# Cross-attention and FFN on one core: loads for attention behind those of query weights, the residual inside the output sums

## The chip, the cores and the metric

The kernel runs on one core of one Trainium2 chip. Its time is the device time in microseconds, lower is better. The core has the engines PE (TensorE, matmuls), DVE (VectorE), ACT (ScalarE), POOL (GpSimd) and SP (SyncE, which here issues every DMA). They run beside each other, each through its own list of instructions in order, and wait for each other on semaphores.

## The reference

B = 8 sequences of 128 tokens of width D = 512, a context of the same shape, 32 heads of width 128:

```
h   = layernorm(x)                      # mean and variance of each token
x1  = x + h + attention(rmsnorm(h) * ln_weight, context) @ w_out.T
        # scores = q k^T + position_bias[head], masked; softmax; times v
n   = layernorm(x1)
out = x1 + ((n * in_scale) @ sign(W).T) * out_scale + bias
        # in_scale, out_scale: softmax(n @ gate.T) times two tables of 8 rows
```

All is float32. The residual x + h of a token is x * (1 + rstd) - mean * rstd: one multiplication with res_scale = 1 + rstd and one addition of res_shift = -mean * rstd.

## The kernel before

**Projections.** A matrix of weights in float32 is split into a high and a low part (w_hi, w_lo; ACT makes the high one, DVE or POOL the low one), and so are the activations (c_hi, c_lo for the context, x_hi, x_lo for the input). A product of two tiles is then three matmuls (L1237, L1238, L1239): high by high, low by high, high by low. Keys and queries come in 16 pairs of heads each, values in 16 pieces. These 48 groups stand in a fixed order, first keys and values mixed, at its end four value pieces (numbers 24 to 27), the last four key pairs (28 to 31), then the 16 query pairs (32 to 47). Except for the first two, a group is a 2 by 2 block product computed with 7 products instead of 8 (a Strassen-like scheme). It needs sums of weight tiles (step WS, on POOL, L695 to L700) and sums of activation tiles (T1 to T4, steps CT and XT, on DVE), and it adds the seven products up in a ring of tiles in SBUF with E1 and C11 (ACT, L760 and L764) and E6, E65, C22, C12, C21 (DVE, L947 to L965). One product is two times three matmuls of 128 x 512.

The input x is loaded and normalised, transposed on PE into big_stage, and then summed and split: steps XT (T3, T1, T2, T4: L1026 to L1035) and XX i (x_hi by ACT at L840, x_lo by DVE at L1079). The split of 4 reads T4, and T4 overwrites what the split of 7 reads.

**Loads.** SP walks its own list. WL m, r is one of two 256 KB loads of the weights of pair m (m = 16 is the first query pair; L565). It waits until the tiles that it overwrites have been read: by the sums of pair m - 1 on POOL, by w_lo of pair m - 1, parts 0 and 1 (row 0), and by part 3 of pair m - 2 (row 1). SAVE writes a ring tile of keys or values to HBM (L599, L602), 256 KB each. KV p loads the keys and the values of head pair p back, 1 MB each (L632, L635); BL i loads the position bias of a head, 64 KB (L643); WOL p loads the output weights of a pair, 512 KB (L650); AL loads x again into acc, 2 MB in all (L655); SMALL loads the FFN's bias, tables and gate (L659 to L662), after POOL has cleared two tiles (L727, L728). All of them go through one hardware queue over 16 DMA engines.

**Attention.** For half a batch and one head (a unit, 64 in all): scores S on PE (L1309); DVE adds bias and mask and takes the maximum (L1101, L1104; the sum of bias and mask is BM, on POOL, L717); EXP on ACT (L846); N normalises on DVE (L1109 to L1111); T transposes on PE (L1317) and ACT copies (L854); PV multiplies with the values on PE (L1328) and splits the result on ACT and DVE (L864, L1118). For each pair of heads p, OUT p, b multiplies the result for sequence b with the output weights, and DVE adds it to acc (add_out, L1127). WO p splits these output weights: the high part on ACT (L872), the low part on POOL (L723). PE writes the outputs into two banks in turn; an output waits until the addition of the output before the last has been made. Projections of query pair p + 2 and attention of pair p are interleaved on PE.

**The residual.** RES b (residual, L1085) turns acc[b] from x into x * res_scale + res_shift, eight instructions of 128 x 512 on DVE. The first additions wait for all eight.

**The order.** schedule() writes one list of steps by hand. Every engine walks the same list and takes the steps that concern it, so the list fixes the order on each engine, and a step of one engine that is placed early can block what stands behind it. Products of group n and of group n - 1 alternate: in cycle n, slots 0, 2, 4, 6 hold the products 1, 6, 2, 5 of group n and slots 1, 3, 5 hold the products 7, 3, 4 of group n - 1. put(cycle, slot, ...) places other steps behind the product of a slot. In the diff k = 24 is the group of the first of the last four value pieces, so k + 5, k + 6, k + 7 are key groups 29, 30, 31, and q = 32 is the first query group. Behind cycle q + 1 the list goes on by head pairs; its first part (p == 0) is written out. WL 16 stands in slot 0 of cycle k + 7, WL 17 in slot 0 of cycle q, WL 18 in slot 0 of cycle q + 1.

Of the kernel before, what the change touches and what calls it, by code (L numbers as in the profile page):

```python
# [82 lines left out]
def schedule():  # L83
# [3 lines left out]
    def put(cycle, slot, *found):  # L87
        beside.setdefault((cycle, slot), []).extend(found)
# [79 lines left out]
    put(k + 4, 5, ("XT", "T2"), ("XX", 7))  # L168
    put(k + 5, 1, ("XX", 6))
    put(k + 5, 4, ("XX", 3))  # L170
    put(k + 5, 6, ("XX", 5))
    put(k + 6, 2, ("XT", "T4"), ("XX", 4))
    put(k + 6, 5, ("KV", 0), ("BL", 0), ("BL", 1))
    q = at[QUERIES[0]]
    put(q, 5, ("BM", 0), ("BM", 1))
    put(q, 6, ("KV", 1), ("WOL", 0))

    put(q + 1, 0, ("S", 0), ("EXP", 0), ("SMALL",))
    put(q + 1, 3, ("N", 0), ("BL", 2))
    put(q + 1, 4, ("S", 1))  # L180
    put(q + 1, 6, ("T", 0), ("EXP", 1), ("BM", 2))

    def product(n, i):
        return [("P", n, i), (READ[i], n)] + ([("SAVE", n, READ[i])] if n < NKV and READ[i] in RESULT else [])
# [52 lines left out]
    for p in range(SPLIT // 2):  # L237
# [8 lines left out]
        if p == 0:  # L246

            first = q + 1
            steps += [*product(first, 7), *prod[1], ("WX", m, 2), ("N", 1), ("PV", 0), ("RES", 0), ("RES", 1)]
            steps += [("S", 2), *product(first, 3), ("T", 1), ("EXP", 2), ("BM", 3), ("BL", 3), *prod[6], ("N", 2), ("PV", 1),  # L250
                      ("WO", 0), ("RES", 2), ("RES", 3)]
            steps += [("S", 3), *product(first, 4), *prod[2], ("WX", m, 3), ("T", 2), ("EXP", 3), ("BM", 4), *prod[5], ("N", 3),
                      ("PV", 2), ("WOL", 1), *load, ("RES", 4), ("RES", 5)]
            steps += [("S", 4), *prod[7], *prod[3], ("T", 3), ("EXP", 4), ("BM", 5), ("BL", 4), ("RES", 6), ("RES", 7), *prod[4],
                      *outs(0, 0), ("N", 4), ("KV", 2), *sums, ("PV", 3), *outs(0, 1, 2)]
            continue
# [32 lines left out]
def xattn_ffn(nc, x, ctx_t, mask, pos_bias, ln_w, wq, wk, wv, wo, ffn_w, ffn_bias, gate_t, scales, out):  # L289
# [27 lines left out]
    with ExitStack() as ctx:  # L317
# [6 lines left out]
        def sem(name):  # L324
            return ctx.enter_context(nc.semaphore(name))
# [99 lines left out]
        v_last_res, v_n, v_scales = sem("v_last_res"), sem("v_n"), sem("v_scales")  # L425
        v_vsum, v_vs4, v_xsum, v_res, v_start = sem("v_vsum"), sem("v_vs4"), sem("v_xsum"), sem("v_res"), sem("v_start")

# [508 lines left out]
        def _(dve):  # L936
# [143 lines left out]

            def residual(i):

                dve.wait_ge(d_acc, 16 * (i // HALF + 1))
                dve.wait_ge(v_res, 4)
                dve.tensor_scalar(acc[:, i, :], acc[:, i, :], res_scale[:, i:i + 1], res_shift[:, i:i + 1],  # L1085
                                  ALU.mult, ALU.add).then_inc(v_start, 1)

            def masks():
# [31 lines left out]
            def add_out(p, b):  # L1120
                n = nth_out[p, b]
                dve.wait_ge(pe_out, n)
                if p:
                    dve.wait_ge(v_acc, nth_out[p - 1, b])
                else:
                    dve.wait_ge(v_start, B)
                dve.tensor_tensor(acc[:, b, :], out_bank[n % 2][:], acc[:, b, :], ALU.add).then_inc(v_acc, 1)  # L1127
# [71 lines left out]
            def scale_product(i):  # L1199
# [6 lines left out]
                if i == B - 1:  # L1206
# [6 lines left out]
                  "CT": ctx_sum, "CX": ctx_low, "LN": input_statistics, "RMS": mean_squares, "RMSR": rms_reciprocals, "H": normed,  # L1213
                  "XT": x_sum, "XX": x_low, "RES": residual, "MASK": masks, "S": scores, "N": normalise,
                  "PV": out_low, "OUT": add_out, "ST": ffn_statistics, "LN2": ffn_norms, "LS": normal_scales, "NT": normal_tile,
# [226 lines left out]
```

## Time and profile before

| | us |
|---|---|
| median of 3 runs (870.11 to 871.13) | 870.71 |
| the profiled execution's own time | 868.79 |
| its span, first to last instruction | 867.0 |
| PE busy | 842.7 |
| DVE busy | 634.1 |

The mean granted clock of PE is 0.985 of full speed. An engine's rows give start, duration and what it did; in brackets stands how long the engine was idle before, and what released it. PE rows of consecutive matmuls overlap, since matmuls are pipelined: the distance from start to start is the time that one takes. Times are microseconds from the start of the span.

### The profile page before, as it was taken

Reading aid. Unit: us, or ns where it says so; the run is one execution under the profiler, and the core shown is the slowest. Engines: PE = TensorE matmul, PEld = TensorE weight load, DVE = VectorE, ACT = ScalarE, POOL = GpSimd, SP = SyncE. Lnnn points to the kernel's source line nnn. Section 1 sums busy time; section 2 is a strip of 40 time slices with the busy share of each in tenths; the row PEclk is TensorE's granted clock in tenths of the full one; section 3 lists DMA queues with packets and bytes.
Section 4 is the critical chain, followed back from the end, with each engine's and each line's share of the span. In section 5 each row is a group of like instructions: output and inputs, shape, how many; then the busy total and the mean of one; then the engine's idle time right before and its main releaser. Section 6 shows DMA issues by size and latency. Waiting matters only on the chain.

```text
span 867.0 us, 12861 instructions
## 1 busy us (share of the span) xinstructions
PE 842.7 (97%) x4348; PEld 705.9 (81%) x4348; DVE 634.1 (73%) x1019; ACT 390.2 (45%) x1005; POOL 302.1 (35%) x279
## 2 busy tenths in 40 slices
PE   9999999999999979989999999999999999999887
PEld 8778888888888858778888888888888888888775
DVE  5777845868765955877778677777777786789765
ACT  5532513422522523535544554455455445556642
POOL 2103211112210233525435544544554345433236
PEclk9999999999999999999999999999999999999969
DMA  8364464663453666123134214412431342150002
GB/s 268 132 212 170 152 208 142 204 220 132 146 180 110 216 229 226 60 106 108 70 131 149 97 60 152 149 62 95 149 113 70 125 150 98 58 208 7 1 1 97
DMA packets 60576, 114.07 MB, mean 132 GB/s; under 512 B 5192, under 2 KB 38600, under 8 KB 55264
## 3 DMA queue, kind: packets, MB, share of 16 engines
q1 hardware_dynamic: 60512, 113.25, 37.9%
q8 instruction: 36, 0.59, 0.3%
q14 instruction: 28, 0.23, 0.1%
HBM read 77.58 MB, written 35.65 MB: 131 GB/s over the span
## 4 chain that ended last, share of the span: by engine, by line
PE 84%; DVE 8%; issue 3%; DMA 2%; ACT 2%; SPq 1%; POOL 0%; DVEq 0%; POOLq 0%; ACTq 0%
PE out L1237 9%; PE out L1239 9%; PE out L1238 9%; PE proj L1237 8%; PE proj L1239 8%; PE proj L1238 8%; PE o L1328 6%; PE s L1309 6%; PE s L1237 3%; PE s L1238 3%; PE s L1239 3%; PE t L1317 3%; DMA w_stage<-in_wq 2%; PE proj L1395 1%; PE proj L1396 1%
## 5 line engine op out<-in xcount | busy, mean ns | idle before, releaser
L846 ACT ACTIVATE probs<-probs,neg_max 128x128 f32<-128x128 f32 x256 | 99.7, 391 | 141.2 <-DVE neg_max L1104 141.1
L695 POOL TENSOR_TENSOR w_stage<-w_stage 128x256 f32<-128x256 f32 x30 | 25.3, 844 | 320.8 <-DMA w_stage<-in_wk 131.3
L1127 DVE TENSOR_TENSOR acc<-out,acc 128x512 f32<-128x512 f32 x128 | 87.4, 688 | 43.0 <-PE out L1239 42.7
L707 POOL TENSOR_TENSOR w_lo<-w_stage,w_hi 128x512 fp32r<-128x512 f32 (+1 forms) x52 | 59.3, 1150 | 142.4 <-ACT w_hi L784 142.4
L1237 PE MATMUL proj<-x_hi,w_hi 128*128 128x512 f32 x210 | 89.9, 428 | 9.6 <-DVE w_lo L972 4.2
L1237 PE MATMUL out<-wo_hi,o_hi 128*128 128x512 f32 x224 | 95.3, 426 | 0.7 <-DVE acc L1127 0.6
L1239 PE MATMUL out<-wo_lo,o_hi 128*128 128x512 f32 x224 | 88.2, 394 | 0.0
L1238 PE MATMUL out<-wo_hi,o_lo 128*128 128x512 f32 x224 | 87.6, 391 | 0.0
L1239 PE MATMUL proj<-x_lo,w_hi 128*128 128x512 f32 x210 | 83.6, 398 | 0.0
L1238 PE MATMUL proj<-x_hi,w_lo 128*128 128x512 f32 x210 | 83.0, 395 | 0.0
L717 POOL TENSOR_TENSOR bias_mask<-bias_raw,mask_neg 128x512 f32<-128x512 f32 x64 | 76.8, 1210 | 9.7 <-DVE probs L1101 9.0
L784 ACT ACTIVATE w_hi<-w_stage 128x512 fp32r<-128x512 f32 (+1 forms) x113 | 61.6, 566 | 23.3 <-DMA w_stage<-in_wq 8.5
L1111 DVE TENSOR_TENSOR probs<-probs,inv_sum 128x512 f32<-128x512 f32 x64 | 67.3, 1051 | 2.2
L864 ACT ACTIVATE o_hi<-o 128x512 fp32r<-128x512 f32 x60 | 35.7, 595 | 48.7 <-PE o L1328 48.7
L1118 DVE TENSOR_TENSOR o_lo<-o,o_hi 128x512 fp32r<-128x512 f32 x60 | 41.0, 683 | 20.7 <-ACT o_hi L864 20.7
L1237 PEld LDWEIGHTS proj<-x_hi,w_hi 128*128 128x128 f32 x210 | 40.1, 191 | 16.9 <-issue 4.6
L972 DVE TENSOR_TENSOR w_lo<-w_stage,w_hi 128x512 fp32r<-128x512 f32 (+1 forms) x61 | 40.9, 670 | 17.2 <-ACT w_hi L784 16.5
L1239 PEld LDWEIGHTS out<-wo_lo,o_hi 128*128 128x128 f32 x224 | 42.0, 188 | 9.6
L1237 PEld LDWEIGHTS out<-wo_hi,o_hi 128*128 128x128 f32 x224 | 42.5, 190 | 7.8 <-issue 1.9
L846 ACT ACTIVATION_READ_ACCUMULATOR probs<-probs,neg_max 128x1 f32 x256 | 47.9, 187 | 0.0
L1239 PEld LDWEIGHTS proj<-x_lo,w_hi 128*128 128x128 f32 x210 | 40.0, 190 | 9.3
L1238 PEld LDWEIGHTS out<-wo_hi,o_lo 128*128 128x128 f32 x224 | 42.5, 190 | 6.0
(317 smaller groups left out, 2143.8 us busy)
## 6 DMA issues: line engine op xcount, KB each, us to landing
k_spill<-ring SPq DMA_DIRECT2D x64, 256.0 KB, 2.7
v_spill<-ring SPq DMA_DIRECT2D x64, 256.0 KB, 2.2
w_stage<-in_wk SPq DMA_DIRECT2D x32, 256.0 KB, 3.4
big_stage<-in_wv SPq DMA_DIRECT2D x8, 1024.0 KB, 7.6
k_first<-k_spill SPq DMA_DIRECT2D x8, 1024.0 KB, 7.3
v_first<-v_spill SPq DMA_DIRECT2D x8, 1024.0 KB, 4.9
w_stage<-in_wq SPq DMA_DIRECT2D x32, 256.0 KB, 4.4
k_second<-k_spill SPq DMA_DIRECT2D x8, 1024.0 KB, 6.7
```

The source lines that it names most:

```text
L707: pool.tensor_tensor(lo, staged(m, part), hi.bitcast(F32), ALU.subtract).then_inc(g_wlo, 1)
L717: pool.tensor_tensor(bias_mask[:, j % 2], bias_raw[:, i % 2][:, None, :].to_broadcast([P, HALF, P]), mask_neg[:, halves[half], :], ALU.add ...
L784: act.activation(hi, staged(m, part), ACT.Copy).then_inc(a_whi, 1)
L846: last = act.activation(probs[:, j % 2, b, :], probs[:, j % 2, b, :], ACT.Exp, bias=neg_max[:, col:col + 1], accum_out=row_sum[:, col:col ...
L1111: dve.tensor_tensor(probs[:, j % 2], probs[:, j % 2], inv_sum[:, cols, None].to_broadcast([P, HALF, P]), ALU.mult).then_inc(v_probs, 1)
L1118: dve.tensor_tensor(lo[:, h % 2], o_bank[:], hi[:, h % 2].bitcast(F32), ALU.subtract).then_inc(v_olo, 1)
L1127: dve.tensor_tensor(acc[:, b, :], out_bank[n % 2][:], acc[:, b, :], ALU.add).then_inc(v_acc, 1)
L1237: pe.matmul(to[:], left_hi, right_hi, start=first and n == 0, stop=False, skip_group_check=True)
L1238: pe.matmul(to[:], left_lo, right_hi, start=False, stop=False, skip_group_check=True)
L1239: last = pe.matmul(to[:], left_hi, right_lo, start=False, stop=n == len(pairs) - 1, skip_group_check=True)
L1309: last = pe.matmul(to[:, b * P:(b + 1) * P], queries[:, b * P:(b + 1) * P], keys, start=True, stop=True)
L1328: last = pe.matmul(to[:, b * P:(b + 1) * P], v_tiles[p % 2][:, half * HALF + b, i * P:(i + 1) * P], probs_t[:, j % 2, b * P:(b + 1) * P], ...
```

## The change

- T4 goes from slot 2 of cycle k + 6 to slot 3 of cycle k + 5, and the split that reads it (XX 4) from slot 2 to slot 1 of cycle k + 6.
- KV 0 and the first two bias loads go from slot 5 of cycle k + 6 to slot 1 of cycle k + 7: behind WL 16, and the bias loads first.
- KV 1 goes from slot 6 of cycle q, in front of WOL 0 and WL 18, to slot 1 of cycle q + 1, behind both.
- WO 0, the split of the first output weights, goes from behind PV 1 to slot 3 of cycle q + 1.
- SMALL goes from slot 0 of cycle q + 1 to behind PV 0.
- The eight RES steps go. add_out for p == 0 is acc * res_scale + output and for p == 1 (output + res_shift) + acc, one scalar_tensor_tensor each; it waits for the load of acc and the four scale and shift instructions in place of the eight residuals.

```diff
--- before.py
+++ after.py
@@ -167,16 +167,19 @@
     put(k + 4, 2, ("XT", "T1"), ("XX", 2))
     put(k + 4, 5, ("XT", "T2"), ("XX", 7))
     put(k + 5, 1, ("XX", 6))
+    put(k + 5, 3, ("XT", "T4"))
     put(k + 5, 4, ("XX", 3))
     put(k + 5, 6, ("XX", 5))
-    put(k + 6, 2, ("XT", "T4"), ("XX", 4))
-    put(k + 6, 5, ("KV", 0), ("BL", 0), ("BL", 1))
+    put(k + 6, 1, ("XX", 4))
+
+    put(k + 7, 1, ("BL", 0), ("BL", 1), ("KV", 0))
     q = at[QUERIES[0]]
     put(q, 5, ("BM", 0), ("BM", 1))
-    put(q, 6, ("KV", 1), ("WOL", 0))
-
-    put(q + 1, 0, ("S", 0), ("EXP", 0), ("SMALL",))
-    put(q + 1, 3, ("N", 0), ("BL", 2))
+    put(q, 6, ("WOL", 0))
+
+    put(q + 1, 0, ("S", 0), ("EXP", 0))
+    put(q + 1, 1, ("KV", 1))
+    put(q + 1, 3, ("N", 0), ("BL", 2), ("WO", 0))
     put(q + 1, 4, ("S", 1))
     put(q + 1, 6, ("T", 0), ("EXP", 1), ("BM", 2))
 
@@ -246,12 +249,11 @@
         if p == 0:
 
             first = q + 1
-            steps += [*product(first, 7), *prod[1], ("WX", m, 2), ("N", 1), ("PV", 0), ("RES", 0), ("RES", 1)]
-            steps += [("S", 2), *product(first, 3), ("T", 1), ("EXP", 2), ("BM", 3), ("BL", 3), *prod[6], ("N", 2), ("PV", 1),
-                      ("WO", 0), ("RES", 2), ("RES", 3)]
+            steps += [*product(first, 7), *prod[1], ("WX", m, 2), ("N", 1), ("PV", 0), ("SMALL",)]
+            steps += [("S", 2), *product(first, 3), ("T", 1), ("EXP", 2), ("BM", 3), ("BL", 3), *prod[6], ("N", 2), ("PV", 1)]
             steps += [("S", 3), *product(first, 4), *prod[2], ("WX", m, 3), ("T", 2), ("EXP", 3), ("BM", 4), *prod[5], ("N", 3),
-                      ("PV", 2), ("WOL", 1), *load, ("RES", 4), ("RES", 5)]
-            steps += [("S", 4), *prod[7], *prod[3], ("T", 3), ("EXP", 4), ("BM", 5), ("BL", 4), ("RES", 6), ("RES", 7), *prod[4],
+                      ("PV", 2), ("WOL", 1), *load]
+            steps += [("S", 4), *prod[7], *prod[3], ("T", 3), ("EXP", 4), ("BM", 5), ("BL", 4), *prod[4],
                       *outs(0, 0), ("N", 4), ("KV", 2), *sums, ("PV", 3), *outs(0, 1, 2)]
             continue
         o = p - 1
@@ -423,7 +425,7 @@
         v_fvar, v_rstd, v_rmax, v_routing = sem("v_fvar"), sem("v_rstd"), sem("v_rmax"), sem("v_routing")
         v_y, v_ylo, v_prod, v_stats = sem("v_y"), sem("v_ylo"), sem("v_prod"), sem("v_stats")
         v_last_res, v_n, v_scales = sem("v_last_res"), sem("v_n"), sem("v_scales")
-        v_vsum, v_vs4, v_xsum, v_res, v_start = sem("v_vsum"), sem("v_vs4"), sem("v_xsum"), sem("v_res"), sem("v_start")
+        v_vsum, v_vs4, v_xsum, v_res = sem("v_vsum"), sem("v_vs4"), sem("v_xsum"), sem("v_res")
 
         g_zero, g_ident, g_bm, g_wsum, g_wlo = sem("g_zero"), sem("g_ident"), sem("g_bm"), sem("g_wsum"), sem("g_wlo")
         g_wo_lo, g_xb, g_res, g_clear = sem("g_wo_lo"), sem("g_xb"), sem("g_res"), sem("g_clear")
@@ -1078,13 +1080,6 @@
                 dve.wait_ge(a_xhi, nth_x_split[i])
                 dve.tensor_tensor(x_lo[:, SLOT[i]], X_SOURCE[i], x_hi[:, SLOT[i]].bitcast(F32), ALU.subtract).then_inc(v_xlo, 1)
 
-            def residual(i):
-
-                dve.wait_ge(d_acc, 16 * (i // HALF + 1))
-                dve.wait_ge(v_res, 4)
-                dve.tensor_scalar(acc[:, i, :], acc[:, i, :], res_scale[:, i:i + 1], res_shift[:, i:i + 1],
-                                  ALU.mult, ALU.add).then_inc(v_start, 1)
-
             def masks():
                 dve.wait_ge(d_mask, 16)
                 dve.tensor_scalar(mask_neg[:], mask_u8, -1.0, MASKED, ALU.add, ALU.mult).then_inc(v_mask, 1)
@@ -1120,10 +1115,19 @@
             def add_out(p, b):
                 n = nth_out[p, b]
                 dve.wait_ge(pe_out, n)
-                if p:
-                    dve.wait_ge(v_acc, nth_out[p - 1, b])
-                else:
-                    dve.wait_ge(v_start, B)
+                if p == 0:
+
+
+                    dve.wait_ge(d_acc, 16 * (b // HALF + 1))
+                    dve.wait_ge(v_res, 4)
+                    dve.scalar_tensor_tensor(out=acc[:, b, :], in0=acc[:, b, :], scalar=res_scale[:, b:b + 1], in1=out_bank[n % 2][:],
+                                             op0=ALU.mult, op1=ALU.add).then_inc(v_acc, 1)
+                    return
+                dve.wait_ge(v_acc, nth_out[p - 1, b])
+                if p == 1:
+                    dve.scalar_tensor_tensor(out=acc[:, b, :], in0=out_bank[n % 2][:], scalar=res_shift[:, b:b + 1], in1=acc[:, b, :],
+                                             op0=ALU.add, op1=ALU.add).then_inc(v_acc, 1)
+                    return
                 dve.tensor_tensor(acc[:, b, :], out_bank[n % 2][:], acc[:, b, :], ALU.add).then_inc(v_acc, 1)
 
             def ffn_statistics(b):
@@ -1211,7 +1215,7 @@
             walk({"DW": plain_weights_low, "DX": plain_ctx_low, "E6": e6, "E65": e65, "C22": c22, "C12": c12, "C21": c21, "WX": key_weights_low, "VX": values_low,
                   "VS": value_sums, "VS4": value_last_sum,
                   "CT": ctx_sum, "CX": ctx_low, "LN": input_statistics, "RMS": mean_squares, "RMSR": rms_reciprocals, "H": normed,
-                  "XT": x_sum, "XX": x_low, "RES": residual, "MASK": masks, "S": scores, "N": normalise,
+                  "XT": x_sum, "XX": x_low, "MASK": masks, "S": scores, "N": normalise,
                   "PV": out_low, "OUT": add_out, "ST": ffn_statistics, "LN2": ffn_norms, "LS": normal_scales, "NT": normal_tile,
                   "SCALES": scales_low, "G": logit_maxima, "ROUTE": route, "Y": scale_tiles, "YL": scaled_low, "MP": scale_product})
 
```

## Rows read from the trace of the kernel before

**Rows 1.** The page: busy time of each engine, its share of the span, its instructions.
```profile
PE 842.7 (97%) x4348; PEld 705.9 (81%) x4348; DVE 634.1 (73%) x1019; ACT 390.2 (45%) x1005; POOL 302.1 (35%) x279
```

**Rows 2.** What PE waited for: engine, line waited for, total us, times, longest.
```profile
PE proj L1237 <- DVE w_lo L972: 4.2, 1, 4.2
...
PE proj L1237 <- DVE ring L956: 2.9, 1, 2.9
```

**Rows 3.** By stage: us, busy PE, PEld, DVE, ACT, POOL; clock, DMA share, GB/s.
```profile
320.00:330.00 10.00, 5.82 (x17) 4.41 (x16) 3.36 (x5) 1.89 (x4) 2.90 (x4) 0.66 0.61 221
...
351.00:377.00 26.00, 21.48 (x115) 17.65 (x116) 23.63 (x39) 13.14 (x45) 12.82 (x12) 0.93 0.25 86
...
377.00:409.00 32.00, 32.00 (x182) 27.56 (x181) 22.82 (x39) 14.84 (x47) 11.18 (x10) 1.00 0.28 97
```

**Rows 4.** PE's own rows: start, us, instruction, idle time before it and its releaser.
```profile
310.47 0.47 PE L1237 MATMUL s<-c_hi,w_hi 128*128 128x512 f32 x1 [1.45 <-DVE w_lo L972]
...
324.42 0.76 PE L1237 MATMUL proj<-x_hi,w_hi 128*128 128x512 f32 x1 [4.18 <-DVE w_lo L972]
...
329.25 0.40 PE L1239 MATMUL s<-c_lo,w_hi 128*128 128x512 f32 x1
...
329.48 0.40 PE L1237 MATMUL proj<-x_hi,w_hi 128*128 128x512 f32 x1
...
351.26 0.50 PE L1237 MATMUL proj<-x_hi,w_hi 128*128 128x512 f32 x1 [1.12 <-DVE ring L965]
...
369.15 0.50 PE L1237 MATMUL proj<-x_hi,w_hi 128*128 128x512 f32 x1 [1.39 <-DVE ring L951]
...
374.11 0.80 PE L1237 MATMUL proj<-x_hi,w_hi 128*128 128x512 f32 x1 [2.87 <-DVE ring L956]
...
376.84 0.48 PE L1237 MATMUL out<-wo_hi,o_hi 128*128 128x512 f32 x1
```

**Rows 5.** DVE's T1, w_lo, T4 and its split, then POOL's weight sum.
```profile
285.87 1.22 DVE L1028 TENSOR_TENSOR big_stage<-big_stage 128x1024 f32<-128x1024 f32 x1
...
301.12 0.67 DVE L972 TENSOR_TENSOR w_lo<-w_stage,w_hi 128x512 fp32r<-128x512 f32 x1
...
305.26 1.75 DVE L1035 TENSOR_TENSOR big_stage<-big_stage 128x1024 f32<-128x1024 f32 x1
...
308.14 1.25 DVE L1079 TENSOR_TENSOR x_lo<-big_stage,x_hi 128x1024 fp32r<-128x1024 f32 x1 [1.13 <-ACT x_hi L840]
...
298.88 1.72 POOL L700 TENSOR_TENSOR w_stage<-w_stage 128x256 f32<-128x256 f32 x1
```

**Rows 6.** The chain that ended last, 310 to 325: start, us, what.
```profile
311.77 0.32 SPq L632
...
314.37 8.83 DMA w_stage<-in_wq
```

**Rows 7.** DMA issues with median us to landing (311:313, 326:328); a row of DVE.
```profile
k_first<-k_spill SPq DMA_DIRECT2D x1, 1024.0 KB, 7.2
...
v_first<-v_spill SPq DMA_DIRECT2D x1, 1024.0 KB, 9.4
...
w_stage<-in_wq SPq DMA_DIRECT2D x2, 256.0 KB, 3.1
...
348.67 0.61 DVE L972 TENSOR_TENSOR w_lo<-w_stage,w_hi 128x256 fp32r<-128x256 f32 x1 [3.34 <-ACT w_hi L784]
```

**Rows 8.** The residual's line: ns min/median/max; its sum; POOL beside it.
```profile
L1085 DVE TENSOR_SCALAR acc<-acc,res_scale,res_shift x8: 536/591/2540, 356.5 to 375.0; 128x512 f32<-128x512 f32 x8
...
L1085 DVE TENSOR_SCALAR acc<-acc,res_scale,res_shift 128x512 f32<-128x512 f32 x8 | 7.3, 957 | 0.0
...
362.00 2.40 POOL L723 TENSOR_TENSOR wo_lo<-wo_raw,wo_hi 128x1024 fp32r<-128x1024 f32 x1 [7.58 <-ACT wo_hi L872]
```

**Rows 9.** The form with a scalar, and the plain output addition: ns min/median/max.
```profile
L1074 DVE SCALAR_TENSOR_TENSOR early<-early,rrms x8: 750/752/1107, 196.9 to 273.7; 128x512 f32<-128x512 f32 x8
...
L1127 DVE TENSOR_TENSOR acc<-out,acc x128: 673/691/693, 378.5 to 823.8; 128x512 f32<-128x512 f32 x128
```

## The prediction, made before the changed kernel was run

> **What bounds the kernel now.** The page first [rows 1]: PE is busy 97% of the span, so time can come only from PE's idle time and from stretches where it runs slowly. The list of what PE waited for [rows 2] is short and begins with 4.2 us for w_lo of L972 and 2.9 us for a ring read on DVE; the rest is smaller. The table by stage [rows 3] puts them all in the hand-over from projections to attention: in the 32 us from 377 on PE is busy 32.00 us, in 351 to 377 it is busy 21.48 of 26.00 us while DVE is at 23.63, and in 320 to 330 it is busy 5.82 of 10 us at a granted clock of 0.66. From PE's rows [rows 4], five stalls:
> - A, 1.45 us before 310.47. The product of the last key group waits for w_lo on DVE. DVE was behind the T4 sum (1.75 us) and the split that follows it, which stood 1.13 us for ACT [rows 5].
> - B, 4.18 us before 324.42. The chain [rows 6] goes back through w_lo, w_hi and the load of query weights issued at 314.37, 8.83 us under way. On SP, k_first, v_first and two bias loads were issued in front of it, from 311.77 on. Behind the idle time the granted clock is at its lower level (1.2 of 2.4 GHz): the 11 matmuls from 324.42 to 329.25 take 4.83 us. At the full clock the start-to-start distance is 0.23 us (329.25 to 329.48), so 2.5 us; the low clock costs 2.3 us.
> - C, 1.12 us before 351.26: the C21 read, behind a w_lo that stood 3.34 us, because the next query load was issued behind k_second, v_second and 512 KB of output weights [rows 7].
> - D, 1.39 us before 369.15, and E, 2.87 us before 374.11 plus a low clock until 376.84: 6 matmuls in 2.73 instead of 1.37 us, so 1.36 us. DVE is full here. Eight residual instructions (L1085) take 7.3 us in it, 0.54 us the shortest and 2.54 us the slowest, which runs beside POOL's wo_lo (2.40 us from 362.00) [rows 8].
>
> Together 1.45 + 4.18 + 2.3 + 1.12 + 1.39 + 2.87 + 1.36 = 14.7 us. From 377 on nothing of this kind is left until the tail, and the change touches nothing there except the added outputs.
>
> **T4 and its split move.** T4 goes one group earlier, behind DVE's C12 read at about 297, and its split goes one product earlier, in front of E6. T4 took 1.75 us beside POOL's weight sums, its sister T1 1.22 us without POOL [rows 5]. In the new place POOL is at its weight sums too, the last of them from 298.88 to 300.60 [rows 5], so I take 1.7 us. DVE stood twice for ACT between there and the w_lo of 301.12 [rows 5], some 0.8 us in all; PE's next product waits for that w_lo, which ends 0.9 us later, and PE loses 0.9 us there (bounds: 0.4, if T4 takes 1.22, and 1.7, if no slack is used). The splits and ring reads behind it keep at least 0.6 us of distance to their products, even E6 of the next group, which is now behind the split. In return stall A goes: the C11 read on ACT no longer stands behind x_hi(4) at 307.05, so w_hi comes about 1.0 us and w_lo about 1.5 us earlier, before PE asks for it. Net 1.45 - 0.9, about 0.6 us gained (-0.3 to 1.1). The Trainium skill (SBUF — State Buffer, Who interferes with whom) speaks against this edit: a VectorE instruction with two SBUF inputs contends with a GpSimd one that reads SBUF. 1.75 against 1.22 us agrees; were T4 free of it in its new place, the edit would bring 1.1 instead of 0.6 us.
>
> **Query weights before K and V.** KV 0 and the bias loads go one slot behind. The load (16) then waits for nothing but its tiles: POOL's sums of the group before and DVE's w_lo of that group. SP would get to it where it now issues k_first, at 311.77 [rows 6], and the w_lo comes somewhat earlier than today: I take 311.2, with nothing but saves in the queue. Two such loads with nothing in front land in 3.1 us [rows 7]; with some traffic I allow 4.5: at 314.5 to 316. PE reaches the product at 320.24 - 0.6 = 319.6; ACT can split at 317.5 (its C11 read comes first) and DVE at 318.2. Stall B goes with its low clock: 4.18 + 2.3 = 6.5 us. What is late next: K and V, issued at 315, 2.1 MB. They took 7.2 and 9.4 us [rows 7], so 322 and 324.5; the first score comes at about 330. Query load 17, issued at 318.6 and 320.6 behind them and three saves, lands at about 326; its w_lo is wanted at 328.8. That is 1.3 us of distance, the smallest of this part. If it is lost, PE stalls for 1 to 2 us, up to 4 us with a low clock.
>
> **KV 1, output weights.** SP now issues WOL 0, load 18, then KV 1 behind the first scores. Load 18's row 0 waits for w_lo(17, 1), DVE's work, so it is issued about as now relative to PE (338.2), but with 512 KB instead of 2.5 MB in front: it lands about 4 instead of 9.5 us after issue, and stall C (1.12 us) goes. k_second is wanted only by S 4, some 25 us after its issue, and takes 5.7 us. WO 0 on ACT (1.05 us, L872) stands now in front of the C11 read of query group 1, where ACT waited for PE, and its POOL part (2.40 us) goes where POOL stood for the late load 18; BM 2 behind it is then done about 5 us before S 2 reads it. The memsets and small loads only move; POOL's 1.46 us stand between BM 2 and BM 3, which has 6 us. I take 0 for all of these. Bounds -0.5 and +2, the latter if ACT stands for wo_raw as it stood for load 18, less its idle time.
>
> **Residual in the output sums.** Gone: 8 instructions, 7.3 us, all in the full stretch of DVE. Added: nothing new, 16 additions change their form to one with a scalar. That form took 0.75 us at L1074, the plain addition 0.69 us [rows 9]: 16 x 0.06 = 1.0 us, in a stage where DVE has 9.2 of 32 us idle [rows 3] and PE alternates between two output banks. Taken as 0. No row has this form with a PSUM input; bounds 0.68 and 2.54 us, the slowest L1085. With WO 0 gone too (1.05 us of ACT in front of T 2's copy), I followed DVE and ACT from PE's product at 351.26 on: N 2 ends at +9.4, N 3 at +15.7, S 4 at +17.7, the C22 read that freed PE at 374.07 now at +18.3 us. PE without stalls D and E asks for that bank at +18.15. So 0.15 us of stall E stays, too short for the clock to fall by what stall C shows (1.12 us, granted clock 1.00 behind it). Gain 1.39 + 2.87 + 1.36 - 0.15 = 5.5 us.
>
> **Sum.** 0.6 + 6.5 + 1.1 + 5.5 = 13.7; 0.2 off for small waits that show only when the large ones are gone: 13.5 us. The profiled execution took 868.79 us with a span of 867.0 [rows 1]; it would be 855.3. The median of the runs is 870.71, 1.9 above the profiled one, and I carry the gain over: 857.2 us.
>
> **Rivals.**
> - Part of the gain is handed on (chance 0.25): a smaller stall comes where one went, through load 17, which has 1.3 us of distance, or DVE, which stays nearly full from S 1 to N 3. For it: DVE at 23.63 of 26 us less 7.3 us still leaves 16 of 20 us in use, in bursts. Against: each distance that I followed was positive. Price: one stall as large as E with its low clock, 4.2 us: 861.4 us.
> - The order of issue does not decide when load 16 lands (0.05). For it stands nothing in the rows: k_first at 319.0, v_first at 321.5, the weights at 323.2 [rows 6, 7] landed in order of issue. If transfers issued together shared the queue evenly, 0.5 MB would come with 2.1 MB, B and C would stay: 857.2 + 7.6 = 864.8 us. The Trainium skill (DMA: Bandwidth & Descriptors, Queues, rings and completion order) says that descriptors are consumed in ring order but that completion is not first in, first out; the first half agrees with these landings, and I keep the rival for the second.
> - Slower than before (0.04): the new addition with a PSUM input. Its place is DVE between two outputs of a pair, where PE can run only two banks ahead. At 2.54 us, 16 of them cost 16 x 1.85 = 29.6 us more; if none of DVE's idle time can take it, since it sits elsewhere, 29.6 - 13.5 = 16 us slower, 873 to 887 us. It turns against the change from about 0.69 + 13.5/16 = 1.53 us each without cover.
> - The change does little (0.02): the stalls come from T4's neighbours and other loads, within 0.2%, 869 to 872.4 us.
>
> **How the numbers follow.** The forecast has 0.64, with its own range 855.5 to 859.5 (all stalls gone, 14.7 us, is 856.0; the run-to-run spread is 0.5 us). For 8 in 10, towards the first rival: 855.3 to 862.5. Faster by over 0.2% (1.7 us, about what a measurement of this kernel tells from none) holds the forecast, the first two rivals: 0.94; the same 0.02; slower 0.04.
>
> **What would show it.** Changed kernel: PE's wait for w_lo behind the in_wq load is gone and the granted clock stays 1.00 from 310 to 365; the load of query weights lands in under 5 us; a stall of up to 1.2 us at about 302 from T4; no gap in front of the last key group; the gap before the first output under 0.5 us, and that output starting near 363.3 instead of 376.84; the fused additions at 0.69 to 0.75 us. I would be wrong if the first output starts earlier by much less than 13 us, or if PE has gaps between the first 24 outputs.

## The result and the profile after

The changed kernel takes 859.26 us (median of 4 runs, 857.39 to 859.60), the kernel before 870.59 (870.11 to 871.13): 11.3 us less. The ratio on record is 0.9863, with a 95% interval of 0.9848 to 0.9879. (Here and below it is the recorded ratio; the quotient of the two medians differs from it by up to 0.0014, here it is 0.9870.) The forecast was 857.2 with 855.3 to 862.5. The profiled execution took 857.39 us against 868.79, 11.4 us less. Line numbers of the changed kernel differ by two to five from those before: its matmuls are L1241 to L1243, the scores L1313, w_lo L974 (higher by four or two), DVE's score addition L1096 and normalisation L1104 to L1106 (lower by five).

The page's first lines, to be held against [rows 1]:

```profile
span 855.6 us, 12845 instructions
...
PE 840.8 (98%) x4348; PEld 705.3 (82%) x4348; DVE 630.6 (74%) x1011; ACT 390.4 (46%) x1005; POOL 301.8 (35%) x279
```

PE works as much as before (840.8 against 842.7 us) in a span that is 11.4 us shorter: what went is idle time and time at the low clock. Of what PE waited for in the hand-over, these are now the two largest entries; the 4.2 and 2.9 us of [rows 2] are gone:

```profile
PE s L1313 <- DVE ring L962: 1.1, 1, 1.1
...
PE out L1241 <- DVE w_lo L974: 0.8, 2, 0.5
```

By stage, in the columns of [rows 3] (engines' busy us with counts, then granted clock, DMA share, GB/s):

```profile
320.00:330.00 10.00, 9.71 (x43) 7.77 (x42) 5.56 (x10) 2.77 (x5) 1.54 (x3) 1.00 0.89 291
...
337.00:363.00 26.00, 24.45 (x142) 20.29 (x141) 23.08 (x40) 12.97 (x40) 15.38 (x15) 1.00 0.45 162
...
363.00:395.00 32.00, 32.00 (x179) 27.51 (x180) 22.97 (x39) 15.51 (x51) 12.14 (x10) 1.00 0.25 85
```

From 320 to 330 PE is busy 9.71 of 10 us at the full clock, where it was busy 5.82 at 0.66. In the 26 us in front of the first outputs it is busy 24.45 instead of 21.48 us; DVE is still at 23.08 us, after 23.63. PE's rows, to be held against [rows 4]:

```profile
303.13 0.47 PE L1241 MATMUL out<-c_hi,w_hi 128*128 128x512 f32 x1 [0.47 <-DVE w_lo L974]
...
329.54 0.47 PE L1241 MATMUL out<-x_hi,w_hi 128*128 128x512 f32 x1 [0.29 <-DVE w_lo L974]
...
338.63 1.16 PE L1313 MATMUL s<-k_first,ring 128*128 128x128 f32 x8 [1.12 <-DVE ring L962]
...
362.88 0.50 PE L1241 MATMUL proj<-x_hi,w_hi 128*128 128x512 f32 x1 [0.22 <-DVE ring L958]
...
364.38 0.40 PE L1241 MATMUL out<-wo_hi,o_hi 128*128 128x512 f32 x1
```

Stalls A to E are gone, and the first output starts at 364.38 instead of 376.84. Small waits stand in their place: 0.47 us at 303.13, 0.29 at 329.54, 1.12 at the second score (338.63), 0.21 at 349.12 for normalised probabilities, 0.22 at 362.88.

For all kernels I divide the stretch up to the first output in four: from the product that starts at 289.57 before (289.86 after) to the last key group, from there to the first score, to the third score, to the first output. Each number is the difference of two start times of PE rows, in us:

| kernel | to last key group | to score 1 | to score 3 | to output 1 | sum | median, us |
|---|---|---|---|---|---|---|
| before | 20.90 | 27.21 | 15.96 | 23.20 | 87.27 | 870.59 |
| changed | 20.19 | 20.95 | 15.48 | 17.90 | 74.52 | 859.26 |
| changed, second profile | 20.18 | 20.90 | 15.51 | 17.91 | 74.50 | 859.44 |
| only KV 0 | 20.48 | 21.52 | 16.66 | 23.09 | 81.75 | 864.88 |
| only the residual | 20.49 | 27.31 | 15.88 | 17.36 | 81.04 | 864.65 |
| only KV 1, WO 0, SMALL | 20.36 | 25.55 | 14.56 | 20.05 | 80.52 | 864.81 |
| only T4 | 20.20 | 23.24 | 16.34 | 21.87 | 81.65 | 867.74 |
| changed, residual back | 20.20 | 20.87 | 15.49 | 20.04 | 76.60 | 860.93 |
| changed, WO 0 late | 20.16 | 22.64 | 15.49 | 17.22 | 75.51 | 859.02 |
| changed, KV 1 early | 20.18 | 21.44 | 16.29 | 21.81 | 79.72 | 862.44 |
| changed, KV 0 behind load 17 | 20.20 | 20.40 | 14.54 | 18.88 | 74.02 | 857.82 |
| that with WO 0 late (a) | 20.19 | 20.74 | 14.62 | 17.20 | 72.75 | 856.96 |
| that with T4 later (b) | 19.14 | 20.42 | 14.55 | 17.20 | 71.31 | 856.17 |

The change brings 12.75 us here. Each row is one execution; only the changed kernel was profiled twice. The last column is less exact: one kernel's runs spread over several us, as the last section tells. The medians of the experiments come from three chips, on which the kernel before had 870.69 us (the four on the kernel before), 871.38 (the next four) and 869.08 (the last three).

### The profile page after: what moved, and what is told of

The parts are those of the page before. It is cut to its first block, busy times and chain, and to the rows that moved or that the text cites. A ratio compares the mean times of both kernels' runs of the same rounds, so it can differ in the third digit from the quotient of the medians.

```text
span 855.6 us, 12845 instructions
## 1 busy us (share of the span) xinstructions
PE 840.8 (98%) x4348; PEld 705.3 (82%) x4348; DVE 630.6 (74%) x1011; ACT 390.4 (46%) x1005; POOL 301.8 (35%) x279
## 4 chain that ended last, share of the span: by engine, by line
PE 87%; DVE 7%; issue 2%; ACT 2%; DMA 1%; POOL 0%; DVEq 0%; POOLq 0%; ACTq 0%; SPq 0%
PE out L1241 10%; PE out L1243 10%; PE out L1242 10%; PE proj L1241 8%; PE proj L1243 8%; PE proj L1242 8%; PE s L1313 6%; PE o L1332 6%; PE s L1243 3%; PE s L1241 3%; PE s L1242 3%; PE t L1321 3%; PE t L1360 1%; PE proj L1399 1%; PE s L1289 1%
## 5 line engine op out<-in xcount | busy, mean ns | idle before, releaser
L1131 DVE TENSOR_TENSOR acc<-out,acc 128x512 f32<-128x512 f32 x112 | 76.2, 687 | 36.5 <-PE out L1243 35.8
L1241 PE MATMUL out<-wo_hi,o_hi 128*128 128x512 f32 x224 | 95.1, 425 | 0.6 <-DVE acc L1131 0.6
L1241 PE MATMUL proj<-x_hi,w_hi 128*128 128x512 f32 x210 | 88.5, 422 | 0.2 <-DVE ring L958 0.2
L1243 PE MATMUL out<-wo_lo,o_hi 128*128 128x512 f32 x224 | 88.2, 394 | 0.0
L1243 PE MATMUL proj<-x_lo,w_hi 128*128 128x512 f32 x210 | 82.7, 394 | 0.0
L1106 DVE TENSOR_TENSOR probs<-probs,inv_sum 128x512 f32<-128x512 f32 x64 | 68.1, 1065 | 2.2
L974 DVE TENSOR_TENSOR w_lo<-w_stage,w_hi 128x512 fp32r<-128x512 f32 (+1 forms) x61 | 42.3, 693 | 11.1 <-ACT w_hi L786 10.5
L1243 PEld LDWEIGHTS out<-wo_lo,o_hi 128*128 128x128 f32 x224 | 42.0, 188 | 9.5
L1241 PEld LDWEIGHTS out<-wo_hi,o_hi 128*128 128x128 f32 x224 | 42.3, 189 | 7.7 <-issue 1.6
L856 ACT ACTIVATE probs_t<-t 128x512 f32<-128x512 f32 x64 | 37.5, 586 | 21.0 <-PE t L1321 19.5
L1243 PEld LDWEIGHTS proj<-x_lo,w_hi 128*128 128x128 f32 x210 | 39.4, 188 | 9.0
```

Source lines behind the costliest of these rows:

```text
L974: dve.tensor_tensor(lo, staged(m, part), hi.bitcast(F32), ALU.subtract).then_inc(v_wlo, 1)
L1106: dve.tensor_tensor(probs[:, j % 2], probs[:, j % 2], inv_sum[:, cols, None].to_broadcast([P, HALF, P]), ALU.mult).then_inc(v_probs, 1)
L1241: pe.matmul(to[:], left_hi, right_hi, start=first and n == 0, stop=False, skip_group_check=True)
L1243: last = pe.matmul(to[:], left_hi, right_lo, start=False, stop=n == len(pairs) - 1, skip_group_check=True)
```

## The experiments

**One part at a time, on the kernel before.** First the loads of the first keys and values:

```diff
-    put(k + 6, 5, ("KV", 0), ("BL", 0), ("BL", 1))
+    put(k + 7, 1, ("BL", 0), ("BL", 1), ("KV", 0))
```

> The kernel before with one edit: KV 0 and the first two bias loads behind the first load of query weights. Theory (each stall goes with its own edit): the 4.2 us wait for w_lo and the low clock behind it go, 6.5 us, but load 17 comes late behind K and V and gives back about 1 us at the second score; the 1.1 us before the C21 read and the two stalls behind the residuals stay. First output at about 371 instead of 376.84, time 864.5 to 866. Rival (order of issue does not decide): load 16 lands near 323 as before, time 870 to 871. Second rival (the backlog on DVE alone sets the first output): PE is earlier up to the first scores, but the first output stays within 2 us of 376.8, time 868.5 to 870.5.

Ratio 0.9940 (0.9921 to 0.9959). The stretch to the first score falls from 27.21 to 21.52 us, so the order of issue does decide when load 16 lands. The next stretch grows by 0.70 us: that is load 17, late already with this part alone. The stretch to the first output does not move (23.09), and the first output starts at 372.21, 4.6 us earlier. Both rivals fall.

**Only the residual.** The eight RES steps go and add_out gets its two forms, as in the change's diff.

> The kernel before with one edit: the eight residual instructions gone, the first two output additions with the scale and the shift in them. Theory: the stalls of 1.39 and 2.87 us and the low clock behind the second shrink to under 0.5 us together, 5 us gained; everything up to 351 stays as before, with its 4.18 us wait. First output at about 371.5, time 865 to 866. Rival (the split of the first output weights, 1.05 us on ACT and 2.40 us on POOL beside DVE, makes these stalls): at least 2 us of them stay, time 867.5 to 869.5.

Ratio 0.9931 (0.9910 to 0.9952). The stretch to the first output falls from 23.20 to 17.36 us and nothing else moves by more than 0.41. What PE still waits for in the hand-over on ring reads of DVE is (engine, line waited for, total us, times, longest):

```profile
PE proj L1239 <- DVE ring L965: 1.1, 1, 1.1
...
PE s L1311 <- DVE ring L960: 0.2, 1, 0.2
```

The first is stall C, the second the old 0.2 us at the second score. Stalls D and E are gone, and nothing is left of the 2 us that the rival wanted to stay.

**Only KV 1, WO 0 and SMALL.**

```diff
-    put(q, 6, ("KV", 1), ("WOL", 0))
-    put(q + 1, 0, ("S", 0), ("EXP", 0), ("SMALL",))
-    put(q + 1, 3, ("N", 0), ("BL", 2))
+    put(q, 6, ("WOL", 0))
+    put(q + 1, 0, ("S", 0), ("EXP", 0))
+    put(q + 1, 1, ("KV", 1))
+    put(q + 1, 3, ("N", 0), ("BL", 2), ("WO", 0))
```

(and WO 0 gone from behind PV 1, SMALL behind PV 0)

> The kernel before with these moves alone: KV 1 behind the output weights and load 18, the split of the first output weights into the first scores, the small loads later. Theory: the 1.12 us before the C21 read go, and what the split of the output weights took from DVE and ACT between 360 and 365 goes as well, 0.5 to 1.5 us, but the residuals keep DVE full: 1.5 to 2.5 us gained, time 868 to 869.5. Rival: 5 us gained, since the slow residual instructions (3.84 us for two beside POOL's wo_lo) get fast: time 865 to 866.5.

Ratio 0.9943 (0.9918 to 0.9967): the rival's size. Of 6.75 us in the table, 0.54 are in front of the last key group and 1.66 in the stretch to the first score, which these edits hardly touch: PE stood 3.2 instead of 4.18 us for load 16, and the low clock behind it was shorter. 1.40 us are stall C. 3.15 us lie in front of the first output, and the residual's line shows one reason (ns min/median/max):

```profile
L1086 DVE TENSOR_SCALAR acc<-acc,res_scale,res_shift x8: 530/538/543, 354.4 to 370.6; 128x512 f32<-128x512 f32 x8
```

With POOL's split of the output weights elsewhere, the eight residuals take 0.54 us each, 4.3 us together, instead of the 7.3 of [rows 8]. The other is the clock: one wait of 2.24 us is left there, and the granted clock behind it is 1.00 in this execution, where stall E carried 1.36 us of low clock. The three moves were made together; how the 3.15 us divide between them was not measured.

**Only T4.**

```diff
+    put(k + 5, 3, ("XT", "T4"))
     put(k + 5, 4, ("XX", 3))
-    put(k + 6, 2, ("XT", "T4"), ("XX", 4))
+    put(k + 6, 1, ("XX", 4))
```

> The kernel before with one edit: T4 and its split earlier. Theory: the 1.45 us wait of the last key group goes, about 0.9 us come in front of w_lo at 302, and the query load 16 is not earlier, since SP issues it behind K and V, which wait for nothing new: PE only waits longer for it, so 0 to 0.6 us gained, time 870 to 870.9. Rival: the chain through T4's split to K's and V's loads (SP waits for all splits of x before KV 0) is what sets load 16: 2 us gained, 868.5 to 869.2.

Ratio 0.9980 (0.9958 to 1.0003), not told from no change; the median, 867.74 us, lies below what the theory and the rival had. The trace says more: 0.70 us less to the last key group, and PE's wait for load 16 at 2.6 instead of 4.18 us, which is the rival's size. SP issued k_first 20.6 us behind the table's starting product, before 22.2 us. The saves of group 29, K, V and load 16 stand in SP's list behind a DVE read which stands behind T4's split. PE's waits, and the granted clock (first number behind POOL's) around the two places where it had been low:

```profile
PE proj L1238 <- DVE ring L957: 2.8, 1, 2.8
...
PE proj L1238 <- DVE w_lo L973: 2.6, 1, 2.6
```

```profile
320.00:330.00 10.00, 7.44 (x33) 5.87 (x32) 6.34 (x9) 2.81 (x5) 2.92 (x4) 1.00 0.61 207
...
371.00:374.00 3.00, 3.00 (x15) 2.47 (x16) 2.06 (x5) 1.17 (x6) 1.76 (x2) 1.00 0.00 0
```

Here neither wait, 2.6 nor 2.8 us, was followed by a low clock. In the kernel before, 4.18 and 2.87 us were. Of what the table gives to T4, about 2.3 us to the first score and 1.3 us to the first output are this and not the edit; a part of what it gives to the three moves above is too.

**One part taken back, on the changed kernel.** The residual (the eight RES steps behind PV 0, PV 1, PV 2 and T 3 again, and plain additions):

> The changed kernel with the eight residual instructions back and plain output additions. Before this run the two edits alone had each taken most of the stalls in front of the first output (residuals gone: 376.84 to 370.31; loads and split moved: to 371.2, where the eight residuals took only 0.54 us each). Theory (the residuals were dear because they ran beside POOL's split of the output weights; 7.3 us against 4.3 us): 8 x 0.54 us come back into a nearly full DVE and cost PE 1.5 to 3 us before the first output, without a low clock; time 1.5 to 3 us above the changed kernel. Rival (the residuals cost what they cost before): 5.5 to 6 us and a low clock in front of the first output, time 864 to 866.

Ratio to the kernel before 0.9888 (0.9858 to 0.9918). The stretch to the first output is 2.14 us longer, in one wait:

```profile
PE proj L1239 <- DVE ring L958: 2.2, 1, 2.2
```

So the theory held in its size. In the kernel before, the same eight instructions were worth 5.84 us: there they ran slowly beside POOL, and the wait that they made was followed by a low clock.

**WO 0 back behind PV 1:**

> The changed kernel with the first output weights split behind PV 1, where they were before. Theory (they hurt only through the residuals beside them): 0 to 0.7 us later at the first output, time within 1 us of the changed kernel. Rival (1.05 us on ACT in front of the copy of the transposed probabilities delays PE by itself): 1 to 2 us later.

Ratio 0.9861 (0.9827 to 0.9894). To the first output it is 0.68 us shorter, not longer: with the residuals gone, the early place of this step costs (the same move on the KV 0 version below takes 1.68 us off). The other difference, 1.69 us in front of the first score, is load 17, which was under way for 8.87 us in this execution and 7.17 in the changed kernel's.

**KV 1 back in front of WOL 0 and load 18:**

> The changed kernel with KV 1 back in front of the output weights and load 18. Theory: load 18 lands 5 us later and wo_raw too, and now the split of the output weights on ACT stands in front of the C11 read and waits for it: PE loses 2 to 5 us between the second and the third score, with or without a low clock; time 861 to 865. Rival (this move brought nothing by itself): within 0.7 us of the changed kernel.

Ratio 0.9904 (0.9869 to 0.9938), the sum of the table 5.2 us longer. ACT's row shows what waits, and PE's row where it is paid:

```profile
340.87 1.06 ACT L873 ACTIVATE wo_hi<-wo_raw 128x1024 fp32r<-128x1024 f32 x1 [3.91 <-DMA wo_raw<-in_wo]
...
352.83 0.66 PE L1320 MATMUL t<-ident,probs 128*128 128x128 f32 x4 [2.83 <-DVE probs L1105]
```

ACT stands 3.91 us for the output weights, and the C11 read, load 18's w_hi and the exponentials stand behind it. The loss was expected between the second and the third score; there the stretch grows by only 0.81 us, and 3.91 us come in front of the first output. The new place of WO 0 needs the new place of KV 1.

**KV 0 behind load 17:**

```diff
-    put(k + 7, 1, ("BL", 0), ("BL", 1), ("KV", 0))
+    put(k + 7, 1, ("BL", 0), ("BL", 1))
+    put(k + 8, 1, ("KV", 0))
```

> The changed kernel with the first K and V loads one cycle later, behind load 17 of query weights; the bias loads stay. Theory (load 17, which landed at 328.3 behind K and V, makes the 0.29 us wait for w_lo and through POOL's weight sums and the bias sum the 1.12 us wait of the second score): both waits go, 1.2 us gained at the third score, and k_first lands near 328, before the first score at 331; time 1 to 1.3 us under the changed kernel. Rival (K lands too late): the first score waits, 0 to 2 us lost.

Ratio 0.9851 (0.9816 to 0.9886). Load 17 lands fast (median us to landing of this kernel's two issues from 316 to 327):

```profile
w_stage<-in_wq SPq DMA_DIRECT2D x2, 256.0 KB, 2.9
```

The waits behind it go (0.18 us is left at the second score): 1.48 us less up to the third score. k_first, issued at 323.53 and 6.3 us under way, landed at about 329.8 and not at 328, only 0.4 us before the first score at 330.20. But 0.98 us come back in front of the first output, where PE now waits 1.2 us for normalised probabilities, so the table's sum is only 0.50 us under the changed kernel. POOL's and DVE's rows of that place:

```profile
340.68 2.85 POOL L726 TENSOR_TENSOR wo_lo<-wo_raw,wo_hi 128x1024 fp32r<-128x1024 f32 x1
...
341.79 2.29 DVE L975 TENSOR_TENSOR w_lo<-w_stage,w_hi 128x512 fp32r<-128x512 f32 x1
...
345.93 0.52 POOL L731 MEMSET routing<- 128x512 f32 x1
...
346.02 1.58 DVE L1106 TENSOR_TENSOR inv_sum<-inv_sum,row_valid 128x4 f32<-128x4 f32 x1
...
346.43 1.15 POOL L720 TENSOR_TENSOR bias_mask<-bias_raw,mask_neg 128x512 f32<-128x512 f32 x1
```

A w_lo that takes 0.67 us alone takes 2.29 beside POOL's split of the output weights, and a product of 128 x 4 elements takes 1.58 us beside POOL's next instructions: it starts during a memset and ends when POOL's bias sum ends (347.60 and 347.58).

**The changed kernel again, and two versions with what had been learned:**

> The changed kernel as it is, beside the two versions below on the same chip. Theory: the waits of PE are a matter of order and come again (0.5 us for w_lo at about 303, 0.3 us or more behind load 17, 1.1 us at the second score), while the place of the low clock in the last 50 us moves from one execution to the next: 11 to 12.5 us under the kernel before. Rival (the first profile was a lucky one): load 17 lands so late that PE loses 1.5 us more, 9.5 to 11 us under.

Ratio 0.9886 (0.9866 to 0.9905). The waits came again to 0.1 us. The time was 9.6 us under the kernel before on this chip, below what I expected; that kernel was at 869.08 us here. The number lies in the rival's range, but its mechanism did not come: load 17 cost no more than in the first profile. Why the gain was smaller here stays open; the two intervals (0.9848 to 0.9879, 0.9866 to 0.9905) overlap.

```diff
-    put(q + 1, 3, ("N", 0), ("BL", 2), ("WO", 0))
+    put(q + 1, 3, ("N", 0), ("BL", 2))
```

(on top of the KV 0 edit; WO 0 behind PV 1)

> The changed kernel with KV 0 behind load 17 and the first output weights split behind PV 1. Before this run: with KV 0 alone moved the second score came 1.7 us earlier, but a w_lo took 2.29 us beside POOL's split of the output weights and PE stood 1.2 us for the normalised probabilities. Theory (that split blocks DVE where DVE is full): from the last key group to the first output 52.2 to 52.8 us instead of 54.33, time 1.2 to 2 us under the changed kernel. Rival (DVE is late for another reason): the 1.2 us wait stays, 53.5 us or more, time within 0.7 us.

Ratio 0.9856 (0.9838 to 0.9874), 2.5 us under the changed kernel beside it, more than the 1.2 to 2 expected. From the last key group to the first output it needs 52.56 us: the 1.2 us wait is gone.

```diff
-    put(k + 5, 3, ("XT", "T4"))
-    put(k + 5, 6, ("XX", 5))
+    put(k + 5, 6, ("XX", 5), ("XT", "T4"))
```

> The version above with T4 behind the w_lo that PE waits for at 303 instead of in front of it. Theory: the two waits of 0.3 and 0.5 us around 299 to 303 go and the last key group still starts without a wait: 0.7 us more gained. Rival (T4's split gets late and the w_lo of the last key group with it): the wait in front of the last key group comes back with 0.3 to 1.4 us and nothing is gained.

Ratio 0.9849 (0.9829 to 0.9869), 856.17 us against 859.44 for the changed kernel in the same runs. 1.05 us go in front of the last key group, and from 290 to 375 PE is left with one wait:

```profile
PE s L1313 <- DVE ring L962: 0.2, 1, 0.2
```

This version beats both kernels. That it also beats the version above, 0.8 us by the medians, is within the spread of the runs; for that step the traces speak (1.44 us in the table), not the times.

## Why the prediction came out as it did, step by step

The direction, the stalls and their order were right. 12.75 of 13.7 us came where they were forecast, and the total is 2.1 us over the forecast. The signs came too: the granted clock from 310 to 365 is 1.00, and the first output starts at 364.38, where 363.3 was named. When both kernels were run again (after_again) the gain was 9.6 us, so the total is known less well than its parts.

- **T4: 0.6 forecast, 0.71 measured.** The outcome was right, by two errors that cancelled. DVE's rows from 297 on, then POOL's:

```profile
297.42 1.21 DVE L1037 TENSOR_TENSOR big_stage<-big_stage 128x1024 f32<-128x1024 f32 x1
...
298.55 0.96 DVE L974 TENSOR_TENSOR w_lo<-w_stage,w_hi 128x256 fp32r<-128x256 f32 x1
...
299.44 1.75 DVE L1081 TENSOR_TENSOR x_lo<-big_stage,x_hi 128x1024 fp32r<-128x1024 f32 x1
...
302.31 0.67 DVE L974 TENSOR_TENSOR w_lo<-w_stage,w_hi 128x512 fp32r<-128x512 f32 x1
...
297.58 1.65 POOL L699 TENSOR_TENSOR w_stage<-w_stage 128x256 f32<-128x256 f32 x1
```

T4 took 1.21 us and not 1.7. POOL was at its sums, and there it was POOL's instruction that took 1.65 us (0.74 before at that place), and DVE's next two that took 0.96 and 1.75 us (0.81 and 1.54 before). The slack was not 0.8 us either: the waits for ACT in DVE's rows before, from start to start, are about 0.6 us. T4's 1.13 us from start to start, less 0.6, plus 0.15 and 0.21 on the next two, make the w_lo of 301.12 come 0.9 us later relative to PE, as worked out. Which of the two engines is held varies. The Trainium skill (SBUF — State Buffer, Who interferes with whom) says that the second to issue blocks; T4 started at 297.42 and POOL's sum at 297.58, it was POOL's sum that took longer, and that agrees.
- **Load 16: 6.5 forecast, 6.26 measured.** Both halves held. It landed in 3.1 us, the first row here; the second is load 17:

```profile
w_stage<-in_wq SPq DMA_DIRECT2D x2, 256.0 KB, 3.1
...
w_stage<-in_wq SPq DMA_DIRECT2D x2, 256.0 KB, 7.5
```

- **Load 17: the step that was mis-sized.** I gave it a landing at 326 and 1.3 us of distance. It was issued at 319.6 and 321.1, 0.5 to 1 us later than forecast, and landed at 328.3, since K and V, two bias loads and three saves went first and the queue needed 7.5 us, not 5.5. The chain's DMA row, POOL's weight sum and bias sum, and DVE's first score addition:

```profile
321.14 7.17 DMA w_stage<-in_wq
...
328.38 0.73 POOL L697 TENSOR_TENSOR w_stage<-w_stage 128x256 f32<-128x256 f32 x1 [10.39 <-DMA w_stage<-in_wq]
...
331.34 2.73 POOL L719 TENSOR_TENSOR bias_mask<-bias_raw,mask_neg 128x512 f32<-128x512 f32 x2
...
333.04 0.69 DVE L1096 TENSOR_TENSOR probs<-s,bias_mask 128x512 f32<-128x512 f32 x1 [1.11 <-POOL bias_mask L719]
```

w_lo is late and PE waits 0.29 us for it. The dearer path was one that I had not followed: POOL takes the bias sum BM 0 only after the weight sums of load 17, so DVE's score addition waits 1.11 us for it, and the C12 read behind it makes PE wait 1.12 us at the second score. The prediction says nothing of BM 0 behind load 17. This is the first rival in small, 1.4 us of waits instead of 4.2. kv0_behind_17 shows the cause: with load 17 in front the first wait goes and the second falls to 0.18 us.
- **Load 18: 1.1 forecast.** Stall C is gone, but with the second score's wait against it only 0.48 us of that stretch remain. "Taken as 0" for KV 1 and WO 0 was right as a sum, wrong as an explanation. Moving WO 0 costs 0.68 us in the changed kernel; in the kernel before, it and the two moves made with it were worth 3.15 us in front of the first output.
- **The residual: 5.5 forecast, 5.30 measured.** Of stall E 0.22 us stay, where 0.15 were worked out. The fused additions cost what was taken (ns min/median/max), and the rival by which they make the kernel slower falls:

```profile
L1123 DVE SCALAR_TENSOR_TENSOR acc<-acc,res_scale,out x8: 737/747/748, 366.0 to 382.8; 128x512 f32<-128x512 f32 x8
...
L1128 DVE SCALAR_TENSOR_TENSOR acc<-out,res_shift,acc x8: 735/750/754, 395.1 to 412.5; 128x512 f32<-128x512 f32 x8
```

How the 5.3 us divide was not as I told it. Residuals without the early WO 0 bring 5.84 us, the early WO 0 with the residuals 3.15, and both 5.30. The parts overlap: the four edits alone add up to 24.1 us in the table's sums, together they bring 12.75. (Some 3.6 us of the 24.1 are the low clock that did not come in the one profiled execution of only T4.)
- **The rest, 1.4 us in the profiled pair, lies outside the stretch.** 0.3 us had been lost before 290, where the kernels do the same; in all profiles together that product starts between 289.3 and 290.7. The other part is in the tail, from the last transpose of probabilities on. Before and after, with the granted clock third from the right:

```profile
809.56:862.71 53.15, 49.20 (x239) 38.60 (x240) 32.76 (x69) 25.68 (x57) 25.27 (x19) 0.87 0.08 31
```

```profile
797.09:851.27 54.18, 50.93 (x239) 40.44 (x240) 32.83 (x69) 25.83 (x57) 25.29 (x19) 0.84 0.08 30
```

Before it takes 53.15 us at a mean clock of 0.87, after 54.18 at 0.84, with the same waits but for 0.9 us less on one for ACT (1.3 before, 0.4 after). The prediction carried this stretch over unchanged. Its length goes with the clock and not, as far as the thirteen profiles show, with an edit: from that transpose to the end of the span it is 57.4 us in four of them at a clock of 0.87 (the kernel before, only KV 0, WO 0 late, KV 1 early), 57.9 to 58.9 in eight at 0.84 and 59.3 in one at 0.81; the last is the changed kernel again, which had 58.5 the first time. So this part of the miss I count as chance.

## What to carry to other kernels

In the one queue of this kernel, an early transfer that was not yet needed delayed the urgent ones behind it (8.83 against 3.1 us to land): order the issues by when they are wanted, and follow each load through every engine that stands in line behind it, a helper engine's sums included. A stall in front of a full engine has more than one remover, so gains of edits measured alone must not be added; and when one remover makes another superfluous, look whether that one now costs something (WO 0 did). A stall of 2.8 us on PE carried a low clock in some executions and not in others: cost it as a chance.

## What the runs showed of the hardware that was not expected

**The spread goes with the low clock.** The first four experiments share 31 runs of the kernel before. Grouped by the mean granted clock of the run: 0.980, 873.1 us (mean of 5 runs); 0.984, 870.3 us (12 runs); 0.988, 867.8 us (4 runs); the ten runs at other values lie in line with these. Waits of 2.6 and 2.8 us were followed by the full clock in one profile (only T4), one of 2.87 us by 1.2 GHz in another. The same wait, 2.76 us for the same ring read, was followed by the low clock with only KV 0 moved (six matmuls in 2.7 us) and by the full one with only T4 moved:

```profile
369.49 0.79 PE L1237 MATMUL proj<-x_hi,w_hi 128*128 128x512 f32 x1 [2.76 <-DVE ring L956]
```

```profile
370.82 0.50 PE L1238 MATMUL proj<-x_hi,w_hi 128*128 128x512 f32 x1 [2.76 <-DVE ring L957]
```

The four runs of the changed kernel, which has no such wait there, had 0.988 to 0.990. So what the removed stalls are worth depends on the execution: against 859.26 us, the three groups give estimates of 13.8, 11.0 and 8.5 us. Whether the removed stalls are the whole difference between the two spreads was not tested, and why the tail's low clock moves stays open.

**A small DVE instruction can be held for over a microsecond.** The 128 x 4 product took 0.16 us in the median of its 64 places and 1.58 us beside POOL. What counted was not its work, but POOL's. It had started 0.41 us before the bias sum of POOL with which it ended, so it was not simply held by an instruction that POOL had begun first; by what rule it was held was not tested, and POOL's times in a profile are rough.
